# Multiplying y by its gate on VectorE straight out of PSUM, in a Mamba and SwiGLU layer on one core

## The chip, the cores and the metric

The kernel runs on 1 core of one Trainium2 chip. The metric is the device time of the launch in microseconds: the kernel before takes 1881.15 us (median of 3 runs, 1876.93 to 1884.44).

## What is computed

One layer over x of 4 sequences x 2048 tokens x 256 features: a Mamba block with residual and layer norm, then a SwiGLU block with residual and layer norm. Cut to what matters here:

```python
x_in, res = jnp.split(x @ W_in, 2, axis=-1)          # 256 -> 2 x 512
u = silu(causal_dw_conv(x_in, conv_w, conv_b))       # u, [tokens, 512]
dt, Bm, Cm = jnp.split(u @ W_x, [16, 32], axis=-1)
delta = softplus(dt @ W_dt + b_dt)
h_t = exp(delta * A) * h_{t-1} + delta * Bm * u      # 512 channels x 16 states
y = sum_n(h * Cm) + u * D
x = layernorm(x + (y * silu(res)) @ W_out)           # the product y * silu(res) is what moves
h2 = silu(x @ wg.T) * (x @ wu.T)
x = layernorm(x + h2 @ wd.T)
```

## The kernel before

The 8192 tokens are cut into 16 chunks of T = 512. The kernel runs in 16 steps. A step has 64 **beats** (NH = 64), one for each pair of state n (16) and block m of 128 channels (4): beat 4n + m. At each beat ScalarE computes da = exp(A * delta) (L1013, into one of two PSUM banks), GpSimd computes dbu = du * B (L1150, four buffers ahead), and VectorE runs the scan of 128 x 512 (L1310). TensorE turns the h of each state in pieces of 128 tokens, so that C, now a value per partition, can weigh it: tokens 0 to 255 of a chunk (the "upper" half) go through `ht_upper`, ScalarE weighs them (L1022) and TensorE turns them back (L699) into the banks `y_upper`, which sum y over the states. Tokens 256 to 511 (the "lower" half) go through `ht_lower`, and VectorE adds them to `acc` in SBUF (L1322). Once `acc` is complete, TensorE turns it into two fill banks, `yt0` and `yt1`.

While step i scans chunk i, the four compute engines also do the **front** of chunk i + 1 (in-projection xin and res, convolution conv, dtb, ct, dt) and the **back** of chunk i - 1 (yt, out-projection o, x1t, gate, up, down). All of these matrix products are called fills. They take turns in 2 PSUM banks in the order of the table `FILL_AT`, which gives the beat of each part of each fill on TensorE; `READ_AT` gives the beat at which another engine reads the bank (a bank is filled again only after that); `BEAT` places what is neither. Within a beat TensorE first issues the turns due (`TURN_AT`, `BACK_AT`) and then the fills; VectorE issues scan, sum, back; ScalarE issues exp, weigh, back, front. Each engine works through its own list strictly in order, so the tables say what stands before what, and the times follow from waits on semaphores.

In ScalarE's list are two places where the table of activation functions is changed and changed back ("silu uz" for u and z, "silu gate" for the SwiGLU gate). The exps of the two beats behind such a place are computed before it, into `da_ahead` in SBUF.

The part at issue, in the step after the chunk's scans: ScalarE copies both banks of `y_upper` into `kb` at beat 6 (L938 through L849) and the banks `yt0` and `yt1` at beats 8 and 10. GpSimd then multiplies each quarter of `kb` by z = silu(res) in place (L1173, beats 11, 12, 12 and 15), and TensorE's out-projections wait for that (`upper_done`, `lower_done`). The last chunk has its own tail, in which VectorE multiplies by z out of PSUM (L1255); the change doesn't touch it. Chunks 0 to 14 go through the part at issue, in steps 1 to 15.

Of the kernel before, what the change touches and what calls it, by code (L numbers as in the profile page):

```python
# [11 lines left out]
ALU = mybir.AluOpType  # L12
# [3 lines left out]
T = 512  # L16
TT = T // P
# [8 lines left out]
FILL_AT = {"xin0": (0, 0), "xin1": (1, 2), "xin2": (2, 2), "yt0": (6,), "xin3": (7, 7), "yt1": (8,),  # L26
# [20 lines left out]
TURN_AT, WEIGH_AT, ADD_AT, BACK_AT = (4, 4, 6, 7), (5, 7), (5, 7), (7, 9)  # L47
# [3 lines left out]
READ_AT = {"conv0": 14, "conv1": 20, "conv2": 22, "conv3": 26, "ct": 48, "down0": 55, "down1": 57, "down2": 63,  # L51
# [4 lines left out]

BEAT = {"times u": [53, 55, 58, 63], "x1 low": [33, 34], "mean": [22, 65], "rstd": [23, 65], "shift": [26, 86],
        "norm": [29, 86], "silu uz": 35, "silu gate": 45, "y upper": [6, 6], "times z": [11, 12, 12, 15]}
# [42 lines left out]
def mamba_swiglu(nc, x, x_t, w_in, conv_w, conv_b, w_x, w_dt, b_dt, a_log, d_skip, w_out, w_gate_t, w_up_t,  # L101
# [31 lines left out]
    with ExitStack() as ctx:  # L133
# [90 lines left out]
        upper_copied, lower_copied = sem("upper_copied"), sem("lower_copied")  # L224
# [230 lines left out]
        def _(pe):  # L455
# [10 lines left out]
            for pair in range(2):  # L466
                taken[f"yt{pair}"] = (lower_copied, DP, pair + 1)
# [224 lines left out]
            def turn_back(i, par, n, k):  # L692


                if n == 0 and k == 0:
                    after(pe, upper_copied, i * DP)
# [150 lines left out]
        def _(act):  # L847
# [88 lines left out]
            def copy_y(pair, times, y):  # L936

                return copy(kb[:, 2 * pair:2 * pair + 2, times], y.rearrange("p (m t) -> p m t", m=2))  # L938

            def back(c, par, beat):  # L940
                for pair in tiles_due("y upper", beat):

                    act.wait_ge(res2_done, TT * (c + 1))
                    act.wait_ge(gt_back, (c + 1) * NUP)
                    copy_y(pair, slice(0, HALF), y_upper[pair]).then_inc(upper_copied, 1)
                for name in due(K_FILLS, beat):
                    n = int(name[-1])
                    b = fill_bank(name)
                    if name[:2] == "yt":
                        act.wait_ge(kp_ready, c * NK + K_AT[name] + 1)  # L950
                        copy_y(n, slice(HALF, T), b).then_inc(lower_copied, 1)
                    elif name[:3] == "x1t":

                        act.wait_ge(kp_ready, c * NK + K_AT[name] + 1)
# [503 lines left out]
```

## Time and profile before

| | |
|---|---|
| median of 3 runs | 1881.15 us (1876.93 to 1884.44) |
| profiled execution, its time / its span | 1876.93 us / 1875.1 us |
| PE (TensorE matmul) busy | 1719.1 us, 92% |
| DVE (VectorE) busy | 1703.1 us, 91% |
| ACT (ScalarE) busy | 1642.7 us, 88% |
| POOL (GpSimd) busy | 1644.9 us, 88% |
| granted TensorE clock, mean | 0.974 of full speed |

All engines are busy for nearly the whole span, and alike in every step, so the page's shares don't say which of them sets the time. One step in the middle has to be read closely: the step whose scans begin at 936.8 us and end with the next step's first scan at 1049.0 us. Beat 0 is at 936.8 in it; its beat 38 is at 1001.7 and its beat 48 at 1020.3. "x4" behind a row says that four like instructions in a row are merged into it. A matrix product of float32 leaves two records for each instruction of the program.

### The profile page before, as it was taken

How to read it: one execution, taken by the hardware profiler on the slowest of the kernel's cores; microseconds unless marked ns; L12 is line 12 of the kernel's file. 1: busy time of each engine (PE TensorE's matmuls, PEld its weight loads, DVE VectorE, ACT ScalarE, POOL GpSimd, SP SyncE). 2: the span in 40 equal slices, each digit the busy share in tenths (PEclk: the TensorE clock that was granted, in tenths of full speed). 3: DMA queues.
4: the chain of work that ended last, by engine and by line, in shares of the span. 5: the costliest groups of instructions: out<-in, count | busy, mean ns of one | idle time of the engine just before them, and what ended most of it. 6: DMA issues, size and time to landing. Idle time of an engine off the chain costs nothing.

```text
span 1875.1 us, 32484 instructions
## 1 busy us (share of the span) xinstructions
PE 1719.1 (92%) x10128; PEld 1289.6 (69%) x10128; DVE 1703.1 (91%) x1953; ACT 1642.7 (88%) x2777; POOL 1644.9 (88%) x1620
## 2 busy tenths in 40 slices
PE   7879898998989999898998989999898998988788
PEld 3546676776767777676776767677676776767577
DVE  4988999999999999999999999999999999999994
ACT  4897998989899898998989899898998989898774
POOL 2889899898999989899898999989899898989970
PEclk8999999999999999999999999999999999999999
DMA  7312214041231313214041231313214141221100
GB/s 245 125 46 107 75 57 146 36 146 47 91 113 60 133 47 120 85 57 146 35 147 54 84 113 66 127 46 128 76 57 146 35 147 58 91 96 40 58 23 24
DMA packets 82107, 165.60 MB, mean 88 GB/s; under 512 B 9857, under 2 KB 27521, under 8 KB 81938
## 3 DMA queue, kind: packets, MB, share of 16 engines
q1 hardware_dynamic: 80786, 161.43, 25.1%
q10 hardware_dynamic: 1152, 2.10, 0.3%
q8 instruction: 85, 1.39, 0.3%
q14 instruction: 84, 0.69, 0.1%
HBM read 87.47 MB, written 8.91 MB: 51 GB/s over the span
## 4 chain that ended last, share of the span: by engine, by line
PE 66%; ACT 22%; POOL 5%; issue 5%; DVE 2%; ACTq 0%; DMA 0%; DVEq 0%; SPq 0%; POOLq 0%
PE fill L509 10%; PE ht_upper L674 9%; PE ht_lower L674 9%; PE y_upper L699 8%; PE fill L614 8%; PE fill L583 5%; PE fill L604 5%; ACT da L1013 4%; POOL dbu L1150 4%; PE fill L524 3%; ACT gt L1022 3%; ACT L1107 2%; ACT L1096 2%; PE fill L553 2%; ACT kb L909 2%
## 5 line engine op out<-in xcount | busy, mean ns | idle before, releaser
L1150 POOL TENSOR_TENSOR dbu<-du,brep 128x512 f32<-128x512 f32 x1024 | 1311.2, 1306 | 167.2 <-DVE h L1310 139.8
L1310 DVE TENSOR_TENSOR_SCAN h<-da,carry,dbu 128x512 f32<-128x512 f32 x960 | 1187.4, 1270 | 96.9 <-ACT da L1013 95.2
L1013 ACT ACTIVATE da<-delta,a_s 128x512 f32<-128x512 f32 x960 | 655.4, 689 | 92.2 <-DVE h L1310 85.6
L1022 ACT ACTIVATE gt<-ht_upper,ct 128x512 f32<-128x512 f32 x512 | 348.4, 680 | 61.6 <-PE ht_upper L674 54.7
L674 PE MATMUL ht_upper<-ident,h 128*128 128x128 f32 x2048 | 318.1, 279 | 67.6 <-DVE h L1310 55.8
L674 PEld LDWEIGHTS ht_upper<-ident,h 128*128 128x128 f32 x2048 | 246.5, 143 | 184.6 <-DVE h L1310 100.1
L1322 DVE SCALAR_TENSOR_TENSOR acc<-ht_lower,ct,acc 128x512 f32<-128x512 f32 x480 | 348.7, 727 | 23.1 <-PE ht_lower L674 23.1
L674 PE MATMUL ht_lower<-ident,h 128*128 128x128 f32 x2048 | 317.2, 278 | 38.7 <-DVE acc L1322 34.2
L699 PE MATMUL y_upper<-ident,gt 128*128 128x128 f32 x2048 | 317.6, 279 | 1.8 <-ACT gt L1022 1.8
L674 PEld LDWEIGHTS ht_lower<-ident,h 128*128 128x128 f32 x2048 | 243.9, 143 | 102.3 <-issue 49.8
L699 PEld LDWEIGHTS y_upper<-ident,gt 128*128 128x128 f32 x2048 | 246.5, 144 | 74.4 <-ACT gt L1022 41.6
L509 PE MATMUL fill<-xt_s,win_s 128*128 128x512 f32 x456 | 219.1, 598 | 0.3 <-DMA win_s<-w_in 0.2
L614 PE MATMUL fill<-wd_s,kb 128*128 128x256 f32 x720 | 180.5, 380 | 0.7 <-DVE xr L1222 0.5
L614 PEld LDWEIGHTS fill<-wd_s,kb 128*128 128x128 f32 x720 | 125.6, 190 | 19.4 <-DVE xr L1222 8.2
L604 PE MATMUL fill<-x1t,wg_s 128*128 128x512 f32 x360 | 129.5, 474 | 3.1 <-ACT kb L961 3.0
L583 PE MATMUL fill<-wout_s,kb 128*128 128x256 f32 x480 | 118.5, 380 | 0.0
L604 PE MATMUL fill<-x1t,wu_s 128*128 128x512 f32 x360 | 110.3, 429 | 4.2 <-ACT delta L891 4.1
L509 PEld LDWEIGHTS fill<-xt_s,win_s 128*128 128x128 f32 x456 | 77.3, 192 | 52.1 <-issue 50.8
L1310 DVE TENSOR_TENSOR_SCAN h<-da_ahead,carry,dbu 128x512 f32<-128x512 f32 x64 | 99.7, 1595 | 0.0
L583 PEld LDWEIGHTS fill<-wout_s,kb 128*128 128x128 f32 x480 | 87.6, 190 | 10.4 <-issue 0.4
L604 PEld LDWEIGHTS fill<-x1t,wg_s 128*128 128x128 f32 x360 | 69.6, 222 | 16.5 <-ACT kb L961 9.1
L297 POOL TENSOR_TENSOR du<-delta,u 128x512 f32<-128x512 f32 x60 | 76.5, 1276 | 4.7
(193 smaller groups left out, 1870.5 us busy)
## 6 DMA issues: line engine op xcount, KB each, us to landing
brep<-b_rows SPq DMA_DIRECT2D x127, 512.0 KB, 3.7
xs<-xin SPq DMA_DIRECT2D x242, 256.0 KB, 2.5
xr<-x SPq DMA_DIRECT2D x16, 512.0 KB, 4.3
xt_s<-x_t SPq DMA_DIRECT2D x15, 512.0 KB, 5.0
out<-xr SPq DMA_DIRECT2D x15, 512.0 KB, 3.9
win_s<-w_in SPq DMA_DIRECT2D x2, 512.0 KB, 5.2
h<-xin SPq DMA_DIRECT2D x4, 256.0 KB, 4.7
h<-xin ACTq DMA_DIRECT2D x4, 256.0 KB, 5.2
```

What stands on the lines that cost most here:

```text
L297: unit.tensor_tensor(du[:, par, m, :], d, u[:, par, m, :], ALU.mult).then_inc(du_ready, 1)
L509: mm = nc.tensor.matmul(front_bank(c, name)[:, :], win_s[:, k, m * P:(m + 1) * P], xt_place(c)[:, k, :], start=(k == 0), stop=(k == KK - 1))
L583: mm = nc.tensor.matmul(fill_bank(name)[:, 0:DM], kb[:, m, t * P:(t + 1) * P], wout_s[:, m, :], start=(m == 0), stop=(m == DB - 1))
L604: mm = nc.tensor.matmul(fill_bank(name)[:, :], w[:, k, n * P:(n + 1) * P], x1t[:, half, k, :], start=(k == 0 and half == 0), stop=(k == KK ...
L614: mm = nc.tensor.matmul(fill_bank(name)[:, 0:DM], kb[:, n, t * P:(t + 1) * P], wd_s[:, n, :], start=(n == 0), stop=(n == HB - 1))
L674: mm = nc.tensor.transpose(bank[:, m * P:(m + 1) * P], h[:, n % 2, m, t * P:(t + 1) * P], ident[:, :])
L699: mm = nc.tensor.matmul(y_upper[m // 2][:, (m % 2) * HALF + k * P:(m % 2) * HALF + (k + 1) * P], lhsT=gt[:, (n * UPPER + k) % GT, m * P:(m ...
L1013: nc.scalar.activation(dst[:, :], delta[:, par, m, :], ACT.Exp, scale=a_s[:, m, n:n + 1])\
L1022: nc.scalar.activation(gt[:, (n * UPPER + k) % GT, :], ht_upper[:, :], ACT.Copy, scale=ct[:, par, k, n:n + 1])\
L1150: nc.gpsimd.tensor_tensor(dbu[:, beat % DBU, :], du[:, par, m, :], brep[:, n // PIECE % 2, n % PIECE, :], ALU.mult).then_inc(dbu_ready, 1)
L1310: nc.vector.tensor_tensor_scan(h[:, n % 2, m, 0:T], da[beat % 2][:, :] if slot is None else da_ahead[:, slot, :], dbu[:, beat % DBU, :], c ...
L1322: nc.vector.scalar_tensor_tensor(out=acc[:, par, k, :], in0=ht_lower[:, :], scalar=ct[:, par, UPPER + k, n:n + 1], in1=acc[:, par, k, :], ...
```

## The change

VectorE reads y in PSUM and writes y * z into `kb` with one `tensor_tensor` of 128 x 512 for each quarter (two of the upper half at beat 5, two of the lower half at beat 6). ScalarE's four copies and GpSimd's four multiplications are gone, with their two semaphores. The tables are another plan of the same work: the fills of xin move from beats 0 to 2 to beats 2 and 3, yt from 6 and 8 to 5 and 5, conv0 and conv1 from 12 and 16 to 9 and 13, o1 from 14 to 13 with its reading from 15 to 13, the first turn of the lower half in each state from beat 4 to 5 (of each four), gate0 is read at 37 and not at 38, and "silu gate" moves from beat 45 to 43 while dtb is still read at 46.

```diff
-FILL_AT = {"xin0": (0, 0), "xin1": (1, 2), "xin2": (2, 2), "yt0": (6,), "xin3": (7, 7), "yt1": (8,),
-           "o0": (9, 9, 11, 11), "conv0": (12,), "o1": (14, 14, 14, 14), "o2": (15, 15, 17, 17), "conv1": (16,),
-           "o3": (19, 19, 19, 19), "conv2": (20,), "res0": (22, 22), "res1": (22, 23), "conv3": (25,),
-           "res2": (26, 27), "res3": (27, 29), "x1t0": (28,), "x1t1": (31,), "gate0": (36, 37), "gate1": (37, 37),
-           "gate2": (39, 39), "gate3": (39, 39), "gate4": (40, 41), "gate5": (42, 43), "dtb": (43, 44, 45, 45),
-           "up0": (45, 46), "up1": (47, 47), "ct": (47,), "dt0": (47,), "up2": (49, 49), "up3": (49, 49),
-           "dt1": (50,), "up4": (51, 51), "up5": (51, 51), "dt2": (52,), "down0": (53, 54, 54, 54, 54, 55),
-           "down1": (55, 55, 56, 56, 58, 58), "dt3": (58,), "down2": (58, 59, 59, 59, 60, 60),
-           "down3": (60, 62, 62, 62, 62, 63)}
+FILL_AT = {"xin0": (2, 2), "xin1": (2, 2), "xin2": (3, 3), "yt0": (5,), "yt1": (5,), "xin3": (7, 8),
+           "o0": (7, 7, 9, 10), "conv0": (9,), "o1": (13, 13, 13, 13), "conv1": (13,), "o2": (14, 15, 16, 17),
+           "o3": (18, 18, 18, 18), "conv2": (21,), "res0": (22, 22), "res1": (23, 23), "res2": (23, 25),
+           "conv3": (26,), "res3": (27, 29), "x1t0": (28,), "x1t1": (30,), "gate0": (35, 37), "gate1": (37, 37),
+           "gate2": (38, 38), "gate3": (39, 39), "gate4": (39, 40), "gate5": (40, 40), "up0": (42, 44),
+           "dtb": (42, 43, 45, 45), "up1": (45, 45), "ct": (47,), "dt0": (47,), "up2": (48, 48), "up3": (49, 49),
+           "dt1": (50,), "up4": (50, 51), "up5": (52, 52), "dt2": (53,), "down0": (54, 54, 54, 54, 55, 55),
+           "down1": (55, 57, 57, 58, 58, 58), "dt3": (57,), "down2": (59, 59, 59, 60, 61, 62),
+           "down3": (62, 62, 62, 62, 62, 62)}
...
-TURN_AT, WEIGH_AT, ADD_AT, BACK_AT = (4, 4, 6, 7), (5, 7), (5, 7), (7, 9)
+TURN_AT, WEIGH_AT, ADD_AT, BACK_AT = (4, 5, 6, 7), (5, 7), (5, 7), (7, 9)
...
-READ_AT = {"conv0": 14, "conv1": 20, "conv2": 22, "conv3": 26, "ct": 48, "down0": 55, "down1": 57, "down2": 63,
-           "down3": 63, "dt0": 49, "dt1": 51, "dt2": 55, "dt3": 59, "dtb": 46, "gate0": 38, "gate1": 39, "gate2": 40,
-           "gate3": 42, "gate4": 42, "gate5": 44, "o0": 12, "o1": 15, "o2": 18, "o3": 20, "res0": 24, "res1": 25,
-           "res2": 28, "res3": 31, "up0": 47, "up1": 47, "up2": 49, "up3": 49, "up4": 51, "up5": 51, "x1t0": 30,
-           "x1t1": 33, "xin0": 2, "xin1": 4, "xin2": 4, "xin3": 9, "yt0": 8, "yt1": 10}
...
-BEAT = {"times u": [53, 55, 58, 63], "x1 low": [33, 34], "mean": [22, 65], "rstd": [23, 65], "shift": [26, 86],
-        "norm": [29, 86], "silu uz": 35, "silu gate": 45, "y upper": [6, 6], "times z": [11, 12, 12, 15]}
+READ_AT = {"conv0": 13, "conv1": 15, "conv2": 22, "conv3": 28, "ct": 47, "down0": 55, "down1": 58, "down2": 63,
+           "down3": 63, "dt0": 49, "dt1": 52, "dt2": 55, "dt3": 59, "dtb": 46, "gate0": 37, "gate1": 38, "gate2": 39,
+           "gate3": 40, "gate4": 41, "gate5": 42, "o0": 11, "o1": 13, "o2": 19, "o3": 19, "res0": 23, "res1": 24,
+           "res2": 27, "res3": 30, "up0": 44, "up1": 45, "up2": 48, "up3": 49, "up4": 51, "up5": 52, "x1t0": 29,
+           "x1t1": 32, "xin0": 2, "xin1": 4, "xin2": 5, "xin3": 10, "yt0": 6, "yt1": 6}
+
+BEAT = {"times u": [52, 57, 61, 63], "x1 low": [33, 33], "mean": [21, 65], "rstd": [21, 65], "shift": [23, 75],
+        "norm": [24, 83], "silu uz": 35, "silu gate": 43, "y upper": [5, 5]}
...
@@ scalar (ScalarE)
-            def copy_y(pair, times, y):
-
-                return copy(kb[:, 2 * pair:2 * pair + 2, times], y.rearrange("p (m t) -> p m t", m=2))
...
@@ gpsimd (GpSimd)
-            def times_z(c, par, k):
...
-                nc.gpsimd.tensor_tensor(kb[:, blocks, times], kb[:, blocks, times], z[:, par, blocks, times], ALU.mult)\
-                    .then_inc(upper_done if k < DP else lower_done, 1)
...
@@ vector (VectorE)
+            def gate_y(par, pair, times, y, done):
+
+                blocks = slice(2 * pair, 2 * pair + 2)
+                nc.vector.tensor_tensor(kb[:, blocks, times], y.rearrange("p (m t) -> p m t", m=2),
+                                        z[:, par, blocks, times], ALU.mult).then_inc(done, 1)
+
             def back(c, par, beat):
+                for pair in tiles_due("y upper", beat):
+
+                    dve.wait_ge(z_ready, max(c + 1, 2))
+                    dve.wait_ge(gt_back, (c + 1) * NUP)
+                    gate_y(par, pair, slice(0, HALF), y_upper[pair], upper_done)
                 for name in due(K_FILLS, beat):
                     n, m = K_AT[name], int(name[-1])
-                    if name[:2] == "up":
+                    if name[:2] == "yt":
+                        dve.wait_ge(kp_ready, c * NK + n + 1)
+                        gate_y(par, m, slice(HALF, T), fill_bank(name), lower_done)
+                    elif name[:2] == "up":
```

## Rows read from the trace of the kernel before

**Rows 1.** All instructions of L900, one per step: ns, first and last start.

```profile
L900 ACT ACTIVATE u<-u x15: 1911/1912/1915, 96.3 to 1669.6; 128x2048 f32<-128x2048 f32 x15
```

**Rows 2.** Busy time by stretch: PE, PEld, DVE, ACT, POOL, granted clock, DMA.

```profile
983.90:1003.90 20.00, 14.58 (x91) 11.72 (x88) 18.00 (x19) 19.84 (x28) 17.17 (x16) 0.91 0.25 79
...
1022.50:1096.10 73.60, 73.37 (x442) 55.37 (x443) 69.94 (x85) 63.85 (x120) 72.69 (x75) 1.00 0.31 108
936.80:1049.00 112.20, 105.47 (x630) 79.70 (x629) 105.05 (x121) 102.07 (x174) 103.81 (x103) 0.98 0.26 90
```

**Rows 3.** The chain that ended last, 936.8 to 1049.0: start, us, what.

```profile
945.02 0.44 PE y_upper L699 x4
...
958.79 1.73 PE fill L583 x8
...
983.94 0.69 ACT gt L1022
...
1001.71 0.52 ACT kb L961
1002.22 0.58 ACT da L1013
1002.80 0.61 ACT gt L1022
...
1015.61 0.67 ACT xd L880
...
1022.05 0.50 ACT delta L891
...
1022.59 1.20 PE fill L604 x4
```

**Rows 4.** Waits from 936.8 to 1049.0: us in total, times, longest.

```profile
DVE h L1310 <- ACT da L1013: 5.7, 8, 2.0
...
PE ht_upper L674 <- DVE h L1310: 2.4, 1, 2.4
...
DVE acc L1322 <- PE ht_lower L674: 1.4, 2, 0.8
```

**Rows 5.** Timeline of DVE in that step: start, us, what [idle before].

```profile
940.44 2.46 DVE L1310 TENSOR_TENSOR_SCAN h<-da,carry,dbu 128x512 f32<-128x512 f32 x2 [0.58 <-ACT da L1013]
943.49 0.75 DVE L1322 SCALAR_TENSOR_TENSOR acc<-ht_lower,ct,acc 128x512 f32<-128x512 f32 x1 [0.60 <-PE ht_lower L674]
944.16 3.62 DVE L1310 TENSOR_TENSOR_SCAN h<-da,carry,dbu 128x512 f32<-128x512 f32 x3
948.00 1.28 DVE L1310 TENSOR_TENSOR_SCAN h<-da,carry,dbu 128x512 f32<-128x512 f32 x1 [0.21 <-ACT da L1013]
949.76 2.46 DVE L1310 TENSOR_TENSOR_SCAN h<-da,carry,dbu 128x512 f32<-128x512 f32 x2 [0.48 <-ACT da L1013]
...
975.43 0.75 DVE L1322 SCALAR_TENSOR_TENSOR acc<-ht_lower,ct,acc 128x512 f32<-128x512 f32 x1 [0.78 <-PE ht_lower L674]
976.44 2.46 DVE L1310 TENSOR_TENSOR_SCAN h<-da,carry,dbu 128x512 f32<-128x512 f32 x2 [0.26 <-ACT da L1013]
...
991.85 0.68 DVE L1244 TENSOR_TENSOR x1t<-fill,kb 128x512 fp32r<-128x512 f32 x1
992.45 1.27 DVE L1310 TENSOR_TENSOR_SCAN h<-da,carry,dbu 128x512 f32<-128x512 f32 x1
...
1001.74 2.46 DVE L1310 TENSOR_TENSOR_SCAN h<-da,carry,dbu 128x512 f32<-128x512 f32 x2 [1.97 <-ACT da L1013]
...
1020.27 2.46 DVE L1310 TENSOR_TENSOR_SCAN h<-da,carry,dbu 128x512 f32<-128x512 f32 x2 [1.49 <-ACT da L1013]
```

**Rows 6.** Groups of instructions by form: busy us, mean ns of one.

```profile
L1310 DVE TENSOR_TENSOR_SCAN h<-da_ahead,carry,dbu 128x512 f32<-128x512 f32 x64 | 99.7, 1595 | 0.0
...
L1173 POOL TENSOR_TENSOR kb<-kb,z 128x512 f32<-128x512 f32 x60 | 75.9, 1278 | 0.0
...
L849 ACT ACTIVATE kb<-y_upper 128x512 f32<-128x512 f32 x30 | 16.1, 592 | 0.0
```

More of the change, by code:

```diff
@@ L223, in mamba_swiglu @@
         lower_done, res1_done = sem("lower_done"), sem("res1_done")
-        upper_copied, lower_copied = sem("upper_copied"), sem("lower_copied")
         high_cut, high_ready, low_ready = sem("high_cut"), sem("high_ready"), sem("low_ready")
@@ L466, in _ @@
             for pair in range(2):
-                taken[f"yt{pair}"] = (lower_copied, DP, pair + 1)
+                taken[f"yt{pair}"] = (lower_done, DP, pair + 1)
             taken["dtb"] = (xd_ready, 2, 2)
@@ L695, in turn_back @@
                 if n == 0 and k == 0:
-                    after(pe, upper_copied, i * DP)
+                    after(pe, upper_done, i * DP)
                 pe.wait_ge(gt_ready, i * NUP + n * UPPER + k + 1)
@@ L934, in reciprocal_std @@
                 nc.scalar.activation(rstd[:, :], rstd[:, :], ACT.Exp, scale=-0.5).then_inc(rstd_step, 1)
-            def copy_y(pair, times, y):
-                return copy(kb[:, 2 * pair:2 * pair + 2, times], y.rearrange("p (m t) -> p m t", m=2))
             def back(c, par, beat):
[L941 to L945, printed above, removed]
                 for name in due(K_FILLS, beat):
@@ L948, in back @@
                     b = fill_bank(name)
[L949 to L952, printed above, removed]
+                    if name[:3] == "x1t":
                         act.wait_ge(kp_ready, c * NK + K_AT[name] + 1)
@@ L1162, in normalise @@
                                             ALU.mult, ALU.add).then_inc((x1_ready, o_ready)[which], 1)
-            def times_z(c, par, k):
-                if k < DP:
-                    pool.wait_ge(z_ready, max(c + 1, 2))
-                    pool.wait_ge(upper_copied, c * DP + k + 1)
-                else:
-                    pool.wait_ge(lower_copied, c * DP + k - DP + 1)
-                blocks, times = slice(k % DP * 2, k % DP * 2 + 2), slice(0, HALF) if k < DP else slice(HALF, T)
-                nc.gpsimd.tensor_tensor(kb[:, blocks, times], kb[:, blocks, times], z[:, par, blocks, times], ALU.mult)\
-                    .then_inc(upper_done if k < DP else lower_done, 1)
             def save_carry(i, n, ends):
@@ L1200, in step @@
                         normalise(i - 2, par, which)
-                    for k in [] if first else tiles_due("times z", beat):
-                        times_z(i - 1, 1 - par, k)
                     for m in [] if last else tiles_due("times u", beat):
```

## Prediction

> **What bounds the kernel now.** I first took the length of a step. The silu of u at L900 stands once in each step; 15 of them start from 96.3 to 1669.6 us, which is 112.4 us for each of 14 steps [rows 1]. A middle step gives 112.2 [rows 2]. Fifteen steps contain the back part, so what the change does to one step counts 15 times.
>
> Busy time by stretch comes next. In the 112.2 us of the step TensorE is busy 105.47, VectorE 105.05, ScalarE 102.07 and GpSimd 103.81 [rows 2], so no engine has more than 10 us to spare and the shares alone decide nothing. The chain of waits orders it: TensorE alone carries it for 73.6 us, from its fill after the reading of dt0 (1022.59, beat 49) to the same place as 983.94 one step on, and its row shows 73.37 us busy there. In the same stretch VectorE is busy 69.94 us, so it has 3.66 us of idle time. Then ScalarE carries the chain through the first change of tables (983.94 to 1003.90, 19.84 busy of 20.0), and after another piece of TensorE through the second one, up to the reading of dt0 [rows 2, 3]. In short: TensorE, then ScalarE, and VectorE just behind both.
>
> The timeline of VectorE shows where its idle time lies. At beat 2 it waits 0.58 for ScalarE, at beat 3 0.60 for TensorE's turn of the lower half, at beats 7 and 8 0.21 and 0.48 for an exp, at 23 0.78 for a turn and at 24 0.26 for an exp; at beats 38 and 48, behind the changes of tables, it waits 1.97 and 1.49 [rows 5]. All its waits for exps are 5.7 us [rows 4], so 0.7 more lies elsewhere. TensorE's own idle time is mostly one wait of 2.4 us for a scan and one of 1.4 for an addition to `acc` [rows 4]; both are around beats 33 to 35, where it has no fill ready. There VectorE sets TensorE's pace.
>
> **The change, part by part.** GpSimd loses four multiplications in a step, 4 x 1.278 = 5.1 us [rows 6]. VectorE is never shown waiting for GpSimd in this step [rows 4], so I value this at 0. ScalarE loses four copies of 0.59 us, 2.4 us in all [rows 6]. What that is worth is the waits of VectorE at beats 7 and 8, right behind those copies: 0.69 us. Later ScalarE waits for others anyway.
>
> VectorE gains four operations of 128 x 512 with one operand in PSUM. The nearest row is L1244, the same kind of operation from a PSUM bank and SBUF: it lasts 0.68 us but the next scan starts 0.60 after it (991.85 to 992.45) [rows 5]. So 4 x 0.60 = 2.4 us; if the overlap were lost, 2.7. That they could be stretched by GpSimd is bounded by the scans that read both operands in SBUF, 1.6 us against 1.27 [rows 5, 6]: 0.3 us each would make 3.7. I take 2.4, since PSUM holds one operand, as in L1244.
>
> The Trainium skill ("GPSIMD Engine Reference", section Key points) says that GpSimd contends with VectorE's instructions only when these have two SBUF inputs or run in a two-port mode. By it the sum is with 2.4; if it failed here, with 3.7. The slower scans out of `da_ahead` agree with it.
>
> Do the new operations wait? In this step TensorE's last turn back into `y_upper` ends at 945.46 [rows 3], while VectorE finishes its third scan from 944.16, that of beat 6, at 947.78 and so that of beat 5 at about 946.5 [rows 5]. So the upper quarters are there 1 us before VectorE asks. A yt fill is four records of 256 columns, half of the eight that take 1.73, and four turns of 0.44 together [rows 3]; two fills need 2 x (0.87 + 0.44) = 2.6 us of TensorE, while VectorE works 2 x 0.60 + 1.2 on the upper quarters and the scan of beat 6. That is even, and I add nothing. Queued behind the four are the scans of beats 6 and 7, and for these wait TensorE's turns. VectorE is then 2.4 - 0.69 = 1.7 us later than now at beat 9.
>
> The new plan has three more places:
> - o1 is filled and read at the same beat, 13. TensorE needs three turns of 0.44 and 1.73 for the fill [rows 3], 3.05 us and some latency from the scan of beat 11; VectorE gets there after two scans and one addition, about 3.1 us. I add 0.3 (0 to 0.6).
> - gate0 is read at beat 37, before the exp of beat 38 for which VectorE waits 1.97 us: + 0.52 [rows 3, 5]. In return TensorE gets the bank earlier, as gate1 is now read before the exp and the weighing of beat 39, 0.58 + 0.61 = 1.2 us [rows 3].
> - The second change of tables moves to 43, and the copy of dtb into xd (0.67), now between its two silus, falls out of it [rows 3]: - 0.67 of the wait of 1.49.
>
> The rest of the moves I value at 0: they shift fills within the stretch that TensorE carries, whose sum of products stays the same.
>
> **The sum.** Whatever TensorE does, VectorE needs in a step its 105.05 busy, + 2.4 for the new products, + 0.3 at beat 13, and those waits for ScalarE which come from a burst in ScalarE's own list: 1.97 + 0.52 at 38, 1.49 - 0.67 behind the second change, 0.58 at beat 2, about 0.7 elsewhere. That makes 112.3, against 112.2 now. Only if all of the waits at beats 3, 23 and 24 (0.60 + 0.78 + 0.26 = 1.64) take up the added work does it come out at that. They are waits for TensorE, which doesn't get slower, so most should go; TensorE in turn will now and then wait for a scan that comes later. I leave a quarter of them standing, 0.4 us: 112.7, or + 0.5 us for each of 15 steps, + 8 us. From the profiled execution's 1876.93 that is 1885; the median lies 4.2 above that execution, so I give 1889.
>
> **The rivals.** What a measurement here can tell from no change is about 0.5%, 9.4 us.
>
> (a) The forecast, + 0.3 to + 0.9 us a step: 1885 to 1895. Chance 0.44, 0.27 of it inside 0.5%.
>
> (b) VectorE becomes the bound and the waits don't give way. For it: it had 3.66 us of idle time in TensorE's stretch, of which 1.3 are ScalarE's bursts, and it starts a chain in which TensorE has its h late at every turn. Against it: the waits at 3 and 23 are TensorE's. It decides once more than half of those waits stands. Price, at the worst 2.4 + 0.3 + 0.52 = 3.2 us a step, 48 us: 1896 to 1929. Chance 0.23.
> The Trainium skill ("Perfetto Trace Analysis") says that the end of a matrix product in a profile is estimated, not observed. If TensorE's 73.37 us were overstated in this way, this rival would be the likelier one; no row here shows it.
>
> (c) The other side: ScalarE's and TensorE's stretches shorten, and the products vanish in VectorE's idle time. The place is the two changes of tables: TensorE gets gate1's bank 1.2 us earlier, the second is 0.67 shorter, together 1.9 us a step, 28 us, down to 1853. It decides if TensorE's wait of 2.4 us near beat 35 shrinks, now that gate0's first part stands at beat 35 before that turn. Against it is the sum above: with VectorE's waits at 38 and behind the second change in place, VectorE alone needs 112.3. Chance of faster by over 0.5%: 0.20.
>
> (d) The copies and products were off the path and the new ones hide wholly, in the waits at 3, 23 and 24: 1877 to 1885, no change. Chance 0.13. The new plan can't fail to act, as every step runs it.
>
> **The numbers.** Predicted 1889; the likeliest case's own range is 1885 to 1895. Faster 0.20, by (c); within 0.5%, 0.27 of (a) and 0.13 of (d), 0.40; slower 0.17 of (a) and 0.23 of (b), 0.40. The range 1864 to 1912 takes (a), (d), two thirds of (b) and half of (c).
>
> **What would show it.** The step's length from L900: 112.7, with 112.3 or less for (c) and (d), over 113.5 for (b). The product's row: 0.68 us, 60 of them; busy time of VectorE in a step 107.4, of ScalarE 99.7, of GpSimd 98.7. Waits for exps at beats 7 and 8 gone; a wait of some 0.3 for the fill at beat 13; the wait at 38 at about 2.5, that behind the second change under 1; TensorE's waits for scans longer than now. I would be wrong if the products waited for `y_upper` or yt, if they lasted over 0.9 us, or if the waits at 38 fell.

## The result and the profile after

The changed kernel takes 1896.75 us (median of 4 runs, 1895.63 to 1898.72), the kernel before 1880.68 in the same comparison: ratio 1.0093 (1.0080 to 1.0106), 16 us slower. I had forecast 1889, 8 us slower. The direction holds, and the time lies in the wide range of 1864 to 1912, but just above the 1885 to 1895 of the forecast's own case. The forecast size is half of what was measured, so the sum was wrong. The profiled execution after has a span of 1895.9 us, against 1875.1; that of before was the fastest of its runs, which is why 20.8 us stand between the profiles and 16 between the medians.

The page of the changed kernel: span, then busy time of VectorE, ScalarE and GpSimd (their share of the span, instructions).

```profile
span 1895.9 us, 32395 instructions
PE 1728.7 (91%) x10128; PEld 1285.4 (68%) x10128; DVE 1746.4 (92%) x2013; ACT 1609.7 (85%) x2717; POOL 1577.4 (83%) x1560
```

VectorE has 43 us more, ScalarE 33 and GpSimd 67 less. All that was moved did move. One plain step of it, in the columns of [rows 2], and the silu of u once a step, as in [rows 1]:

```profile
949.00:1062.10 113.10, 106.44 (x630) 79.26 (x629) 107.94 (x123) 99.76 (x170) 99.19 (x99) 0.98 0.25 89
...
L898 ACT ACTIVATE u<-u x15: 1912/1913/1917, 98.4 to 1687.3; 128x2048 f32<-128x2048 f32 x15
```

The mean step is 113.5 us, against 112.4. The first scan of each step gives the lengths one by one. After: 116.7, 114.1, **114.4**, 113.0, 113.4, 113.0, 113.0, **114.4**, 113.1, 113.0, 113.0, 113.0, **114.4**, 113.0, 113.0. Before: 111.8, 114.6, then 112.2 ten times, 112.4, 112.5 and 112.9 once each. Of the 20.8 us 0.4 lie before the first scan, 4.9 in the first step, 13.0 in the next fourteen, and 2.5 in the last step with the tail.

VectorE's timeline in that plain step, those rows that wait or are new; beat 0 is at 949.0:

```profile
952.56 2.46 DVE L1296 TENSOR_TENSOR_SCAN h<-da,carry,dbu 128x512 f32<-128x512 f32 x2 [0.43 <-ACT da L999]
957.94 1.26 DVE L1202 TENSOR_TENSOR kb<-y_upper,z 128x512 f32<-128x512 f32 x2
960.31 1.26 DVE L1202 TENSOR_TENSOR kb<-fill,z 128x512 f32<-128x512 f32 x2
986.21 2.47 DVE L1296 TENSOR_TENSOR_SCAN h<-da,carry,dbu 128x512 f32<-128x512 f32 x2 [0.70 <-ACT da L999]
990.67 1.28 DVE L1296 TENSOR_TENSOR_SCAN h<-da,carry,dbu 128x512 f32<-128x512 f32 x1 [0.15 <-ACT da L999]
1014.77 2.46 DVE L1296 TENSOR_TENSOR_SCAN h<-da,carry,dbu 128x512 f32<-128x512 f32 x2 [2.18 <-ACT da L999]
1023.80 1.95 DVE L1296 TENSOR_TENSOR_SCAN h<-da_ahead,carry,dbu 128x512 f32<-128x512 f32 x1
1026.04 0.69 DVE L1219 SCALAR_TENSOR_TENSOR kb<-fill,kb 128x512 f32<-128x512 f32 x1 [0.29 <-ACT kb L907]
1026.64 1.62 DVE L1296 TENSOR_TENSOR_SCAN h<-da_ahead,carry,dbu 128x512 f32<-128x512 f32 x1
1029.99 1.28 DVE L1296 TENSOR_TENSOR_SCAN h<-da,carry,dbu 128x512 f32<-128x512 f32 x1 [0.50 <-ACT da L999]
...
1060.63 0.75 DVE L1308 SCALAR_TENSOR_TENSOR acc<-ht_lower,ct,acc 128x512 f32<-128x512 f32 x1 [0.30 <-PE ht_lower L673]
```

Every wait of [rows 5] between beats 3 and 24 is gone: those at beats 3, 7, 8, 23 and 24. In their place stand new ones: 0.70 at beat 22 and 0.15 at 25 (behind ScalarE's statistics, now at beat 21), 0.29 and 0.50 around the second change of tables instead of 1.49, 0.30 at beat 63. VectorE's idle time in a step falls from 7.15 to 5.15 us (length less busy time), its busy time rises by 2.9 [rows 2]. The four products have 2.4 of that, two rows of 1.26 for two each, less the overlap. The other 0.4 are in the two scans out of the scratch buffer, rows 1023.80 and 1026.64, which took less in the kernel before:

```profile
1013.78 3.16 DVE L1310 TENSOR_TENSOR_SCAN h<-da_ahead,carry,dbu 128x512 f32<-128x512 f32 x2
```

### The profile page after: what moved, and what is told of

Its sections match the earlier page's. It is cut to its first block, busy times and chain, and to the rows that moved or that the text cites. A ratio compares the mean times of both kernels' runs of the same rounds, so it can differ in the third digit from the quotient of the medians.

```text
span 1895.9 us, 32395 instructions
## 1 busy us (share of the span) xinstructions
PE 1728.7 (91%) x10128; PEld 1285.4 (68%) x10128; DVE 1746.4 (92%) x2013; ACT 1609.7 (85%) x2717; POOL 1577.4 (83%) x1560
## 3 DMA queue, kind: packets, MB, share of 16 engines
q8 instruction: 85, 1.39, 0.3%
## 4 chain that ended last, share of the span: by engine, by line
PE 57%; ACT 14%; POOL 11%; DVE 9%; issue 8%; DVEq 0%; DMA 0%; ACTq 0%; POOLq 0%; SPq 0%
POOL dbu L1136 8%; PE ht_upper L673 8%; PE fill L613 8%; PE ht_lower L673 7%; PE y_upper L697 7%; DVE h L1296 7%; PE fill L508 6%; PE fill L582 5%; PE fill L603 5%; PE fill L534 3%; ACT L1093 2%; POOL xr L1147 2%; DVE acc L1308 2%; PE fill L523 2%; ACT kb L926 2%
## 5 line engine op out<-in xcount | busy, mean ns | idle before, releaser
L999 ACT ACTIVATE da<-delta,a_s 128x512 f32<-128x512 f32 x960 | 655.4, 690 | 113.1 <-DVE h L1296 107.2
L673 PEld LDWEIGHTS ht_upper<-ident,h 128*128 128x128 f32 x2048 | 241.3, 142 | 280.5 <-issue 136.4
L613 PE MATMUL fill<-wd_s,kb 128*128 128x256 f32 x720 | 175.5, 380 | 0.4 <-DVE xr L1194 0.2
L582 PE MATMUL fill<-wout_s,kb 128*128 128x256 f32 x480 | 126.0, 380 | 0.5 <-DVE xr L1194 0.5
L603 PE MATMUL fill<-x1t,wu_s 128*128 128x512 f32 x360 | 119.0, 439 | 2.5 <-DVE kb L1219 2.5
L603 PE MATMUL fill<-x1t,wg_s 128*128 128x512 f32 x360 | 116.4, 457 | 0.0
L1296 DVE TENSOR_TENSOR_SCAN h<-da_ahead,carry,dbu 128x512 f32<-128x512 f32 x64 | 106.2, 1680 | 0.0
L582 PEld LDWEIGHTS fill<-wout_s,kb 128*128 128x128 f32 x480 | 82.9, 190 | 13.8 <-issue 7.6
L294 POOL TENSOR_TENSOR delta<-delta,du 128x512 f32<-128x512 f32 x60 | 76.7, 1278 | 10.6 <-ACT delta L893 10.6
```

What stands on the lines that cost most here:

```text
L294: unit.tensor_tensor(d, d, du[:, par, m, :], ALU.add).then_inc(delta_ready, 1)
L582: mm = nc.tensor.matmul(fill_bank(name)[:, 0:DM], kb[:, m, t * P:(t + 1) * P], wout_s[:, m, :], start=(m == 0), stop=(m == DB - 1))
L603: mm = nc.tensor.matmul(fill_bank(name)[:, :], w[:, k, n * P:(n + 1) * P], x1t[:, half, k, :], start=(k == 0 and half == 0), stop=(k == KK ...
L613: mm = nc.tensor.matmul(fill_bank(name)[:, 0:DM], kb[:, n, t * P:(t + 1) * P], wd_s[:, n, :], start=(n == 0), stop=(n == HB - 1))
L673: mm = nc.tensor.transpose(bank[:, m * P:(m + 1) * P], h[:, n % 2, m, t * P:(t + 1) * P], ident[:, :])
L999: nc.scalar.activation(dst[:, :], delta[:, par, m, :], ACT.Exp, scale=a_s[:, m, n:n + 1])\
```

## The experiments

Each kernel was timed in 5 rounds beside the kernel before on the same chip (1879.6 to 1880.5 us there). Step lengths are from the first scans. TensorE's granted clock falls to half once in nearly every step, at beats 34 to 36 or, in some steps, at beat 37 or 38; the latter are called late falls here. "Plain step" is the commonest length of steps 1 to 14 without a late fall, "late" the commonest length of those with one, and how many of the 14 they are.

| | median us | ratio (95%) | plain step | late | first step |
|---|---|---|---|---|---|
| before | 1880.7 | | 112.2 | none | 111.8 |
| the change | 1896.8 | 1.0093 (1.0080-1.0106) | 113.0 | 114.4 (3) | 116.7 |
| e1 old tables, products on VectorE | 1903.9 | 1.0126 (1.0110-1.0142) | 113.8 | none | 113.1 |
| e2 six products | 1924.7 | 1.0237 (1.0219-1.0254) | 114.2 | 115.5 (11) | 116.7 |
| e3 products of few columns | 1897.1 | 1.0091 (1.0074-1.0107) | 112.8 | 114.2 (3) | 116.8 |
| e4 first step's own fills at old beats | 1892.9 | 1.0071 (1.0057-1.0085) | 113.0 | 114.4 (3) | 114.7 |
| e5 gate0 read after the exp | 1906.6 | 1.0137 (1.0120-1.0154) | 113.4 | 115.0 (6) | 117.2 |
| e6 new tables up to x1t only | 1900.4 | 1.0105 (1.0090-1.0120) | 113.4 | none | 114.7 |
| e7 old engines, new tables from gate0 | 1913.0 | 1.0172 (1.0154-1.0189) | 113.6 | 115.2 (8) | 112.8 |
| e8 layer norm at old beats | 1906.2 | 1.0134 (1.0121-1.0147) | 113.3 | 114.8 (6) | 116.7 |
| e9 before, 16 more transposes | 1882.5 | 1.0009 (0.9999-1.0019) | 112.2 | 113.3 (1) | 111.9 |
| e10 the change, 14 more transposes | 1897.2 | 1.0091 (1.0078-1.0104) | 113.0 | 114.4 (5) | 116.1 |
| e11 new tables, old engines | 1923.2 | 1.0224 (1.0211-1.0237) | 114.0 | 115.4 (10) | 116.8 |
| e12 e1 with upper products at 5 | 1901.4 | 1.0111 (1.0097-1.0125) | 113.7 | none | 112.0 |
| e13 e12 with lower products at 7, 9 | 1900.5 | 1.0108 (1.0094-1.0122) | 113.6 | none | 111.9 |
| e14 the change, turns at old beat | 1935.2 | 1.0287 (1.0266-1.0308) | none | 115.7 (14) | 116.8 |
| e15 the change, xin at old beats | 1923.2 | 1.0223 (1.0209-1.0238) | 114.0 | 115.4 (10) | 116.7 |
| e16 before, xin2 at beat 3 | 1882.9 | 1.0016 (1.0007-1.0025) | 112.5 | none | 111.9 |
| e17 before, xin at new beats | 1883.9 | 1.0017 (1.0008-1.0026) | 112.5 | none | 111.7 |

Late falls come in the kernels with the new beats for the gate fills, and otherwise only once, in e9. The section on e9 and e10 shows what they cost.

**e1: the products alone, under the old tables**

```diff
-"y upper": [5, 5], FILL_AT, READ_AT, TURN_AT, BEAT of the change
+"y upper": [6, 6], FILL_AT, READ_AT, TURN_AT, BEAT of the kernel before
```

> The products on VectorE, with every table of the kernel before (products at beats 6, 6, 8 and 10). Theory A (VectorE's 2.4 us of new work in a step are paid by the part that its waits for TensorE and the copies don't take up): the waits at beats 7 and 8 go (0.7), those at 23 and 24 give some 0.5 to 1.0 of their 1.04, so a step is 112.9 (112.5 to 113.3), and the first step, which has no products, stays at 111.8: about 1891 us (1885 to 1897). Rival B (the new tables cost the time, the products are hidden): within 2 us of the kernel before, 1879 to 1883. Rival C (the new tables are what makes the products bearable): a step over 113.5, over 1900 us.

Rival C came true, not theory A: 24 us for the products alone, and a step of 113.8. VectorE's timeline, beat 0 at 948.3:

```profile
955.00 0.75 DVE L1308 SCALAR_TENSOR_TENSOR acc<-ht_lower,ct,acc 128x512 f32<-128x512 f32 x1 [0.60 <-PE ht_lower L673]
959.21 1.26 DVE L1202 TENSOR_TENSOR kb<-y_upper,z 128x512 f32<-128x512 f32 x2
...
988.52 0.75 DVE L1308 SCALAR_TENSOR_TENSOR acc<-ht_lower,ct,acc 128x512 f32<-128x512 f32 x1 [0.87 <-PE ht_lower L673]
989.53 1.28 DVE L1296 TENSOR_TENSOR_SCAN h<-da,carry,dbu 128x512 f32<-128x512 f32 x1 [0.26 <-ACT da L999]
```

The waits at beats 7 and 8 are gone, but those at beats 3, 23 and 24 stand at 0.60, 0.87 and 0.26 as in [rows 5]. They took up nothing. From start to start the two waits at beats 7 and 8 had cost VectorE 0.86 us, so 1.5 of the 2.4 us are left. TensorE has a wait that the kernel before lacks, 19.6 us in 15 times: its first turn back of the next chunk may start only when VectorE has emptied y_upper. Who waited for the products (us, times), and one of the 15:

```profile
  PE y_upper L697: 19.6, 15
...
960.53 0.66 PE L697 MATMUL y_upper<-ident,gt 128*128 128x128 f32 x4 [1.39 <-DVE kb L1202]
```

Compared turn by turn with the kernel before, TensorE is on time up to this turn and 1.6 us late from it on, to the end of the step.

**e12 and e13: other beats for the products, old tables**

```diff
-"y upper": [6, 6], "yt0": 8, "yt1": 10
+"y upper": [5, 5], "yt0": 8, "yt1": 10      # e12
+"y upper": [5, 5], "yt0": 7, "yt1": 9       # e13
```

> The tables of the kernel before with the products on VectorE (1903.9 us when the upper ones stand at beat 6), now with the upper products at beat 5, the lower ones still at 8 and 10. Theory D (those products cost 1.6 us a step because TensorE's first turn back of the next chunk, beat 7, has to wait until VectorE has emptied y_upper, 1.39 us idle): that wait goes, a step is 112.2 to 112.8 instead of 113.8, 1882 to 1890 us. Rival (VectorE's 2.4 us of work are the cause, wherever they stand): 113.4 to 113.8, over 1896 us.

> As the kernel with the upper products at beat 5, and the lower ones at 7 and 9 instead of 8 and 10. Theory D: the wait is the same as with 8 and 10, within 3 us of that kernel. Rival (each product has its own place, and VectorE's beats 7 and 9, of which 9 has an addition as well, are the worse ones): 3 to 10 us slower than that kernel.

Theory D fell, and the rival of e12 came true: TensorE's wait of 1.39 us shrinks to 0.21, yet the step falls only from 113.8 to 113.7. TensorE now waits for another product as well, the one that empties the fill bank for yt1:

```profile
731.72 0.66 PE L697 MATMUL y_upper<-ident,gt 128*128 128x128 f32 x4 [0.21 <-DVE kb L1202]
...
735.84 1.13 PE L574 MATMUL fill<-u,diag_d 128*128 128x256 f32 x4 [0.66 <-DVE kb L1202]
```

The timeline of the kernel before shows no wait of TensorE in beats 0 to 30. In e12 TensorE is 0.4 us late from the first of these rows and 1.5 from the second. In e13 the second one goes, but TensorE then waits for scans that come later (0.25 at one turn), and it is 1.3 us late by beat 12. So the cause is VectorE's work, wherever it stands in this stretch, and it holds up TensorE too. Compared beat by beat with the kernel before, VectorE is 1.5 us late in e12 at beat 11 and still at beat 63. Its rows in e12, beat 0 at 720.7:

```profile
727.37 0.75 DVE L1308 SCALAR_TENSOR_TENSOR acc<-ht_lower,ct,acc 128x512 f32<-128x512 f32 x1 [0.60 <-PE ht_lower L673]
730.40 1.26 DVE L1202 TENSOR_TENSOR kb<-y_upper,z 128x512 f32<-128x512 f32 x2
...
760.85 0.75 DVE L1308 SCALAR_TENSOR_TENSOR acc<-ht_lower,ct,acc 128x512 f32<-128x512 f32 x1 [0.84 <-PE ht_lower L673]
761.86 2.46 DVE L1296 TENSOR_TENSOR_SCAN h<-da,carry,dbu 128x512 f32<-128x512 f32 x2 [0.26 <-ACT da L999]
```

The wait at beat 3 lies in front of the products. The one at 23 lies behind them (0.65 us in e13), but what it waits for, a turn of h and the fills in front of it, comes later by the same amount, since the products have held up TensorE.

**e2 and e3: more and less product work in the change**

```diff
 def gate_y(par, pair, times, y, done):
+    if times.start == 0:                                  # e2: two more of 0.6 us
+        nc.vector.tensor_tensor(kb[:, DB + pair, :]..., y..., z[:, par, blocks, times], ALU.mult)
...
+    few = slice(times.start, times.start + 4)             # e3, from the third step on
+    nc.vector.tensor_tensor(kb[:, blocks, few], y...[:, :, 0:4], z[:, par, blocks, few], ALU.mult)
```

> The changed kernel with 6 instead of 4 products in a step: each upper one is issued a second time into a free block of the scratch tile, so VectorE has 2 x 0.6 = 1.2 us more in each of 15 steps. Theory A (VectorE is at its limit in the changed kernel): all of it is paid, 15 x 1.2 = 18 us, 1915 us (1911 to 1917). Rival B (VectorE still has room, the new tables cost the time): under 6 us more, 1897 to 1903.

> The changed kernel in which, from the third step on, each product takes only 4 columns of each block instead of 256 (this part of the gating is left out), so VectorE has about 4 x 0.5 = 2.0 us less in each of 14 steps; all waits and tables stay. Theory A: a part of it comes back, until TensorE's stretch binds: a step of 112.0 to 112.5 instead of 113.0, 7 to 14 us, 1883 to 1890 us; the first step's 116.7 stays. Rival B (the new tables cost the time): under 3 us less, 1894 to 1897.

e3 leaves out 252 of each 256 columns of the product. In e2 1.2 us more cost 28 us, more than theory A's 18. The plain step is 1.2 longer, as theory A had it: from beat 6 on VectorE is later by that much. The other 10 us are late falls of the clock, 11 and not 3, which add 1.3 us each; why there are more of them is open. In e3 some 2 us less give back 0.2 in a step, so its rival B came true. In the changed kernel the products lie just at the edge: they fill waits that would stand there anyway, and VectorE has no wait left between beats 3 and 21 to take up more. VectorE in e3, beat 0 at 832.7, the products now 0.21 for two:

```profile
841.69 0.21 DVE L1207 TENSOR_TENSOR kb<-y_upper,z 128x8 f32<-128x8 f32 x2
842.59 1.28 DVE L1301 TENSOR_TENSOR_SCAN h<-da,carry,dbu 128x512 f32<-128x512 f32 x1 [0.69 <-ACT da L999]
843.79 0.21 DVE L1207 TENSOR_TENSOR kb<-fill,z 128x8 f32<-128x8 f32 x2
...
846.02 2.46 DVE L1301 TENSOR_TENSOR_SCAN h<-da,carry,dbu 128x512 f32<-128x512 f32 x2 [0.83 <-ACT da L999]
```

Waits of 0.69 and 0.83 us have come up at beats 6 and 8. So 0.6 of the 0.8 us of a plain step stay even with the products nearly gone; they belong to the new tables and the waits around them, 0.2 to the length of the products.

**e6, e7 and e11: halves of the tables, old engines**

```diff
-FILL_AT, READ_AT from gate0 on, "silu gate": 43        (e6: those of before, 45)
+the same into the kernel before                        (e7)
+all new tables, copies at 5, 5, 6, 6, "times z": [9, 9, 10, 10]   (e11)
```

> The changed kernel with the new tables only up to x1t; from gate0 on (change of tables at 45, reads of gate, up and down) those of the kernel before. Theory A (the second half of the new tables saves about as much at dtb's copy as it loses by the slower scans out of the scratch buffer and by gate0's copy; it is neutral in a steady step, but makes the long steps): a step of 113.0 without the three of 114.4 and with a first step of 113 or less, 1888 to 1893 us. Rival B (the second half of the new tables is what lets the products hide): a step of 113.5 or more, over 1902 us.

> The kernel before (copies on ScalarE, products on GpSimd) with the new tables from gate0 on. Theory A: neutral in a steady step (112.0 to 112.4), but with a longer first step and some long ones: 1881 to 1890 us. Rival B (the second half is a gain of its own, since dtb's copy falls out of the change of tables, 0.67 us a step): 1871 to 1876 us.

> All tables of the changed kernel, but ScalarE copies (beats 5, 5, 6, 6) and GpSimd multiplies (its beats 9, 9, 10, 10, some four ahead of VectorE's) as in the kernel before. Theory A (the new tables by themselves lose about 0.6 us in a steady step and 5 in the first, and need the quick product, since o0 is filled at beat 7): the out-projections wait for GpSimd by 1 to 3 us in each step, 1905 to 1935 us. Rival B (the tables are good by themselves and VectorE's products are the whole loss): under 1888 us.

With the products on VectorE the plain step is 113.8 under the old tables (e1), 113.4 with the new first half (e6), 113.0 with both. Each half helps the products by 0.4; e6 lies between its theory and its rival. With the old engines the new second half makes the plain step 1.4 us longer (e7, slower than both theory and rival had it), and all of the new tables make it 1.8 longer (e11); late falls add 1.4 to 1.6 us in over half of the steps. The tables have no worth of their own; they fit one set of durations.

The time of e11 is theory A's, but not the mechanism: TensorE never waits for GpSimd in the out-projections. It is ScalarE's four copies, at beats 5 and 6 in a row, that VectorE waits behind (beat 0 at 730.3):

```profile
741.15 1.28 DVE L1310 TENSOR_TENSOR_SCAN h<-da,carry,dbu 128x512 f32<-128x512 f32 x1 [1.80 <-ACT da L1013]
743.40 1.28 DVE L1310 TENSOR_TENSOR_SCAN h<-da,carry,dbu 128x512 f32<-128x512 f32 x1 [0.97 <-ACT da L1013]
745.17 2.46 DVE L1310 TENSOR_TENSOR_SCAN h<-da,carry,dbu 128x512 f32<-128x512 f32 x2 [0.48 <-ACT da L1013]
```

**e5, e8, e14 and e15: one item of the new tables put back**

```diff
-"gate0": 37, "gate1": 38                        +"gate0": 38, "gate1": 39                       # e5
-"mean": [21, ..], "rstd": [21, ..], norm 24     +"mean": [22, ..], "rstd": [23, ..], norm 29    # e8
-TURN_AT (4, 5, 6, 7)                            +TURN_AT (4, 4, 6, 7)                           # e14
-"xin0": (2, 2), "xin1": (2, 2), "xin2": (3, 3)  +"xin0": (0, 0), "xin1": (1, 2), "xin2": (2, 2) # e15
```

> The changed kernel with gate0 read at beat 38 behind the exp (and gate1 at 39) instead of in front of it at 37. Theory A (the copy of gate0 in front of the exp lengthens VectorE's wait at beat 38): the wait falls from 2.18 to about 1.6 and a step by 0.3 to 0.5, 1890 to 1892 us. Rival B (TensorE's fills gate2 and gate3 then come later, and the turn of beat 40 with them): the wait at 38 falls but returns at beats 40 and 41, no gain, 1895 to 1898; if all long steps (114.4) multiply, over 1898.

> The changed kernel with mean, rstd, shift and norm of the first layer norm at the beats of the kernel before (22, 23, 26, 29, not 21, 21, 23, 24). In the changed kernel VectorE waits 0.70 us for an exp at beat 22, behind ScalarE's statistics of beat 21, and the chain of waits goes through these statistics and GpSimd's normalisation into VectorE's scans. Theory A (this placing costs what is lost in beats 21 to 25): the waits of 0.70 and 0.15 go, a step is 112.4 to 112.8 instead of 113.0, 1888 to 1893 us. Rival B (the burst only moves: the wait stands at beat 24 and TensorE's turn at 23 is late again): no gain, 1895 to 1900.

> The changed kernel with the first turn of the lower half at beat 4 of each state, as in the kernel before, and not at 5. Theory T (turning it later takes nothing from anyone, as the fills moved with it): within 3 us of the changed kernel, 1894 to 1900. Rival U (the later turn is what costs the steady 0.8 us a step): 1884 to 1888 us.

> The changed kernel with the fills of xin0 to xin2 at beats 0 to 2 (as in the kernel before) and not at 2 and 3. Theory T (in the changed kernel all of TensorE's beats 0 to 21 are without idle time, and moving fills within them changes nothing): within 3 us of the changed kernel. Rival V (VectorE then waits 0.6 us at beat 3 again, since the third fill stands before the turn of the lower half): 0.3 to 0.6 us a step, 1901 to 1906 us.

All four made it slower, by 10 to 38 us, against my theory in each, and all but e5 by more than any rival said. Part of that is more late falls. By the plain step e5 costs 0.4 us, e8 0.3 and e15 1.0; e14 has no step without a late fall. In e5 VectorE's wait at beat 38 does fall, from 2.18 to 1.69, but 0.16, 0.25 and 0.25 come up at beats 40 and 41, as its rival B said, and with them more long steps. In e8 the waits of 0.70 and 0.15 go and one of 1.42 stands at beat 24 (beat 0 at 727.4), again as rival B said:

```profile
768.32 2.46 DVE L1296 TENSOR_TENSOR_SCAN h<-da,carry,dbu 128x512 f32<-128x512 f32 x2 [1.42 <-ACT da L999]
```

In e15 the wait at beat 3 is back, at 0.89 us, as rival V said. No single one of these items holds the loss; each is better where the change has it. I had placed 0.52 us on gate0's copy; putting it back costs 0.4.

**e16 and e17: one item of the new tables in the kernel before**

```diff
-"xin2": (2, 2)    READ_AT "xin2": 4
+"xin2": (3, 3)    READ_AT "xin2": 5             # e16; e17: all three xin as in the change
```

> The kernel before with one thing of the new tables: xin2 is filled at beat 3, behind the turn of the lower half, and read at beat 5. Theory L (a wait of VectorE is local: it goes when the fill in front of the turn it waits for is moved, and comes back as step time, while work put elsewhere leaves it as it is): the wait of 0.60 at beat 3 goes, a step is 111.6 to 111.9 instead of 112.2, 1871 to 1876 us. Rival (TensorE's sum of products sets the step, the wait only moves to a later turn): within 2 us of the kernel before.

> The kernel before with xin0 to xin2 filled at beats 2, 2 and 3, as in the new tables. Theory L: the wait at beat 3 gets shorter or goes, but TensorE has no fill at beats 0 and 1 and then waits for ScalarE's weighing; 1871 to 1880 us. Rival (without the products at beats 5 and 6 the later xin fills hold up beat 5 and the yt fills): 1884 us and more.

Theory L, as I put it there, fell too. In e16 the wait of 0.60 at beat 3 goes, and one of 0.83 stands at beat 6 (beat 0 at 714.4):

```profile
724.42 1.28 DVE L1310 TENSOR_TENSOR_SCAN h<-da,carry,dbu 128x512 f32<-128x512 f32 x1 [0.83 <-ACT da L1013]
726.00 1.28 DVE L1310 TENSOR_TENSOR_SCAN h<-da,carry,dbu 128x512 f32<-128x512 f32 x1 [0.30 <-ACT da L1013]
```

So the new tables' use of this is clear: they move VectorE's wait from beat 3, in front of the products, to beats 6 to 8, where a product can fill it. By itself the move gives nothing (+ 0.3 us a step). e17 has the same waits, and comes out at its rival's time.

**e4: the first step**

```diff
+FIRST_RES_FILL = {"gate0": (36, 37), "gate1": (37, 37), "gate2": (39, 39), "gate3": (39, 39)}
+FIRST_RES_READ = {"gate0": 38, "gate1": 39, "gate2": 40, "gate3": 41}
```

> The changed kernel, but the fills of the first step that make its own z stand at the beats of the kernel before (filled at 36 to 39, read at 38 to 41) and not at 35 to 40. The first step is 116.7 us in the changed kernel against 111.8, and by its beat 41 it is already 4.8 late. Theory A (these fills of 0.85 us for each product of 128 x 512, at half the clock behind ScalarE's change of tables, hold up the turns of beats 38 to 41): 2 to 4 us come back, 1893 to 1895 us. Rival B (the first step is long because of the moved convolutions and the clock alone): no difference, 1895 to 1898.

As theory A had it: the medians differ by 3.8 us, the profiles by 2.6, and 2.0 of that is the first step. The changed kernel's timeline there:

```profile
104.69 3.34 PE L621 MATMUL fill<-xt_s,win_s 128*128 128x512 f32 x4
105.18 2.46 DVE L1296 TENSOR_TENSOR_SCAN h<-da,carry,dbu 128x512 f32<-128x512 f32 x2 [3.37 <-ACT da L999]
108.77 0.75 DVE L1308 SCALAR_TENSOR_TENSOR acc<-ht_lower,ct,acc 128x512 f32<-128x512 f32 x1 [1.13 <-PE ht_lower L673]
109.01 1.88 PE L621 MATMUL fill<-xt_s,win_s 128*128 128x512 f32 x4
```

Four records take 3.34 us where the next four take 1.88: the fills stand under the half clock, and VectorE waits 1.13 us for the turn behind them. The other 2.9 us come with the new first half of the tables (e6 has 114.7 without the new gate beats). In e4 VectorE waits 2.01, 0.45, 0.63, 0.63 and 1.58 us for exps at beats 6, 13, 15, 17 and 25 of that step, 5.3 us together, where the kernel before waits 2.9 up to beat 26. Which of the moves brings them is open.

**e9 and e10: TensorE kept at work near beat 35**

```diff
+if beat == KEEP_AT:       # 35; before the fills of the beat
+    wait_bank(i, "gate0")
+    for n in range(KEEP): # 16 (e9), 14 (e10)
+        nc.tensor.transpose(fill_bank("gate0")[:, ...], ident[:, :], ident[:, :])
```

> The kernel before with 16 more transposes of the identity (0.11 us each) at the end of TensorE's beat 35 in each step, into the bank that gate0 fills next, where TensorE waits 2.4 us for a scan. Theory W (the half clock that the trace shows once in each step near beat 35 comes after this idle time): there are fewer stretches of half clock, a step is 0 to 0.6 us shorter, 1870 to 1880 us. Rival (the half clock comes whatever TensorE does there): the stretches stay, and the transposes are slow under it and hold up the turn of beat 36 by up to 1 us: 1881 to 1895 us.

> The changed kernel with 14 more transposes of the identity at TensorE's beat 35, in front of gate0's first part, where TensorE waits 1.9 us for a scan. Theory W (the long steps of 114.4 us are those in which the half clock falls on the gate fills of beats 38 to 40, not on the idle time before): without the half clock the long steps become 113.0 and the first step gets shorter, 1885 to 1892 us. Rival (the half clock stays): 1896 to 1910 us, with more long steps, as the transposes are slow under it.

The half clock does go: the mean granted clock is 0.989 in e9, against 0.974, and of its one stretch in each step near beat 35 one is left in steps 1 to 14. The time stays, 1.0009. Theory W was right on the clock and wrong on the time. A plain step of e9, without the fall, agrees with one of the kernel before, with it, within 0.03 us at every beat, so where the clock falls on idle time it costs nothing. (Six steps of e9 are 0.7 to 1.1 us longer. One has the late fall; in another the delay comes at beat 23, before the transposes. Why is open.)

In e10 five stretches are left, at beats 37 and 38, and just those five of steps 1 to 14 are over 114 us. The change has three such steps, so theory W's gain did not come; the time is the rival's. In the change the three steps of 114.4 are just those with a late fall. VectorE's scans in the step from 949.0 (113.1 us) and in the one of 114.4 before it are within 0.15 us of each other up to beat 40, then 1.0 apart at 41 and 1.3 from 42 to the end. Two stretches of 6 us, 899 to 905 in the step of 114.4 and 1013.4 to 1019.4, the same place of the step from 949.0; the last but two columns give the granted clock:

```profile
899.00:905.00 6.00, 5.72 (x27) 4.94 (x27) 4.29 (x4) 4.66 (x10) 3.73 (x5) 0.72 0.11 43
1013.40:1019.40 6.00, 5.59 (x33) 4.66 (x34) 4.63 (x5) 6.00 (x12) 3.77 (x5) 1.00 0.18 67
```

At 0.72 the gate fills are late, and ScalarE waits for one of them, in front of an exp:

```profile
904.32 0.60 ACT L947 ACTIVATE kb<-fill 128x512 f32<-128x512 f32 x1 [1.34 <-PE fill L603]
```

## Why the prediction was wrong, point by point

Two steps of it failed. The waits for TensorE at beats 3, 23 and 24 did not take up the new work, and the change was priced by one plain step times 15, with the first step and TensorE's clock put at nothing. In the plain step luck hid most of the first; some two thirds of the missing time come from the second.

- **Cost of the products: right.** 0.68 us each by L1202, 0.60 with the overlap, 60 of them; y_upper and yt kept VectorE waiting once, for 0.2 us. ScalarE's share was right too: the 0.69 us at beats 7 and 8 went.
- **"... all of the waits at beats 3, 23 and 24 ... take up the added work", "They are waits for TensorE, which doesn't get slower, so most should go": failed.** e1, e12 and e13 have the products under the old tables, and there these waits stand, 1.5 to 1.7 us together (1.64 before). The products then cost 1.4 to 1.6 us a step, which is 2.4 less the 0.86 that the waits at beats 7 and 8 had cost from start to start. TensorE does get later: it waits for the products to empty its banks, or for the scans behind them, and is 1.3 to 1.6 us late from there on. That a quarter of these waits would stand was a guess.
- **"The rest of the moves I value at 0" failed.** With the old engines they cost 43 us (e11); with the products they are worth 7 us (change against e1). In the change the waits did go from beats 3, 23 and 24, but because the fills in front of those turns were moved, and 0.70 + 0.15 + 0.30 us came up at beats 22, 25 and 63.
- **The three places.** At beat 13 no wait came (0.3 forecast). The wait at 38 is 2.18, not 2.5. Behind the second change of tables 0.50 + 0.29 stand for 1.49, as said (0.82). But the two scans out of the scratch buffer there take 1.95 and 1.62 us, 3.57 together, where in the kernel before the pair took 3.16: + 0.4 that I had not counted. The 1.6 us that I had read for such scans was a mean of two kinds, 1.9 to 2.0 and 1.25, so it was no bound.
- **The plain step** came out at 113.0 (forecast 112.7). That it is only 0.3 off is luck. In the forecast's sum, the waits left standing were 0.4 and measured 1.15 (beats 22, 25, 63), and VectorE's busy time was 0.5 more than forecast. Against that beats 13, 38 and 2 and the waits elsewhere came out 1.0 lower.
- **"... what the change does to one step counts 15 times": failed by more.** The forecast's + 8 us are 15 x 0.5; the profiles differ by 20.8. Of the missing 13 us the first step has 4.9; it has no back part, and I had taken it as untouched. The fourteen steps behind it have 6.0 more than 14 x 0.5: 4.2 by 0.3 in each and 4.1 by three late falls of the clock, which I had left out, less some 2 us, since two long steps of the kernel before got no longer. The last step with the tail has 2.0 more, and 0.4 lie before the first scan; these two I can't explain.
- **Rivals.** (b), that the waits don't give way, came nearest: 1896.8 us is inside its 1896 to 1929, and 1.15 us of waits stand, if at other beats, for 1.64, more than the half at which it decides, though the step is not over its 113.5. VectorE is a bound on one side only: 1.2 us more of its work cost 1.2 us in a plain step (e2), but 2 us less give 0.2 (e3). (c) did not come: the second change of tables got shorter by 0.7 and TensorE's longest wait for a scan fell from 2.4 us to 1.9, as it had asked, and yet the step got longer. (d), no change, is refuted.
- Why each item of the new tables is better where the change has it is not settled beyond the rows shown, nor is why the clock falls late in some steps.

## What to carry to other kernels

In a kernel of in-order engines tied to each other every few microseconds, don't sum up a step's idle time and spend it on new work. Ask of each wait whether the new work stands in front of it, and whether the engine that it waits for will itself wait for the new work. If it does, the wait only moves to a later time and takes up nothing. A plan of beats fits one set of durations, so an engine move must be judged with its own plan. The first and last rounds, where half of the work is missing, must be priced by themselves. Steps of two lengths are to be told apart before a difference of medians is put down to an edit: a third of e2's loss came with the clock and not with VectorE's work.

## What the runs showed of the hardware

TensorE's granted clock fell to half, its lower level (1.2 GHz), once in nearly every step, after TensorE's waits behind beats 33 to 35, for 3.4 or 6.8 us. Where it fell at beats 34 to 36, on idle time, it cost nothing measurable (e9, 1.0009). Where it fell at beat 37 or 38, on fills that others wait for, the step was 1.3 to 1.6 us longer in every kernel with the new gate beats that has both kinds.

A scan whose two inputs both lie in SBUF, out of the scratch buffer, took 1.6 to 2.0 us where a product of GpSimd was under way as it began, and ended 1.1 us after that product. Where none was, it took 1.25, against 1.27 with one input in PSUM. GpSimd was held up as well. Its copy of 128 x 4, 0.19 us at the median, took 1.12 beside the scan from 1023.80 and ended with it, within 0.02 us. In the kernel before, the second scan of the pair from 1013.78 took 1.25 us, and GpSimd's two products beside it took 3.41 us and not 2.50. The first two rows are of the change, the last two of the kernel before:

```profile
1018.61 0.20 POOL L1154 COPY carry<-h 128x4 f32<-128x4 f32 x1
...
1024.62 1.12 POOL L1154 COPY carry<-h 128x4 f32<-128x4 f32 x1
...
1012.20 2.50 POOL L1150 TENSOR_TENSOR dbu<-du,brep 128x512 f32<-128x512 f32 x2 [0.44 <-DVE h L1310]
1015.85 3.41 POOL L1150 TENSOR_TENSOR dbu<-du,brep 128x512 f32<-128x512 f32 x2 [1.16 <-DVE h L1310]
```

The products, with one input in PSUM, had 662 to 692 ns throughout.

This agrees with the Trainium skill ("GPSIMD Engine Reference", section Key points), which names VectorE instructions with two SBUF inputs among those that contend with GpSimd.
